# First pass of a decoder layer: scores of four heads by one product with K on a block diagonal, head average by adding transposes, dt in six buffers

## What is computed

```
x_dbl = xs @ x_proj.T;  dt, Bm, Cm = split(x_dbl)           # 64, 16, 16
dt = softplus(dt @ dt_proj.T + dt_b)                         # 512 channels
h  = exp(dt * A) * h + dt * Bm * xs;  y = sum_n h * Cm       # scan over 128 tokens, 16 states
x  = layernorm(x + (y + D * xs) * silu(z) @ out_proj.T)
Q, K = x @ Wq, ctx @ Wk                                      # 4 heads of 32
scores = where(mask, Q K^T / sqrt(32), -inf)                 # 128 x 128 per head
attn = softmax over the 32 largest of each row, 0 elsewhere
c_t = mean over heads(attn) @ ctx @ Wv ...
```

## Time and profile before

| | us |
|---|---|
| three runs | 7404.6, 7409.21, 7412.53 |
| median | 7409.21 |
| profiled execution | 7415.14 |
| its span, first to last instruction | 7413.3 |
| mean granted clock of TensorE | 0.944 |

### The profile page before, as it was taken

How to read it: one execution, slowest core, us unless ns; L and a number is a source line. 1 busy time by engine, 2 the same in 40 slices (tenths; PEclk the granted TensorE clock), 3 DMA queues, 4 the chain that set the end, 5 groups by cost and what they waited for, 6 DMA issues and landing times. The chain is left out here.

```text
span 7413.3 us, 107688 instructions
## 1 busy us (share of the span) xinstructions
PE 6760.6 (91%) x25104; PEld 3801.7 (51%) x25104; DVE 5403.0 (73%) x13960; ACT 4455.8 (60%) x9788; POOL 4601.7 (62%) x3991
## 2 busy tenths in 40 slices
PE   3899999999999999999999999996899999999996
PEld 1354455444554555544554445543656666555664
DVE  5588888888888888888888888885255555555555
ACT  2788887887878887888878888773211111111111
POOL 0888888888888888888888888883011111111111
PEclk6999999999999999999999999997899999999998
DMA  1666566555666566655666556664511111101010
GB/s 44 136 147 147 136 153 154 145 143 136 154 152 148 142 144 161 147 142 136 151 155 147 142 139 155 153 147 136 189 30 32 32 32 32 30 28 30 28 32 20
DMA packets 554213, 835.19 MB, mean 113 GB/s; under 512 B 169179, under 2 KB 207388, under 8 KB 551712
## 3 DMA queue, kind: packets, MB, share of 16 engines
q1 hardware_dynamic: 552768, 820.23, 44.7%
q10 hardware_dynamic: 864, 8.65, 0.3%
HBM read 745.91 MB, written 74.45 MB: 111 GB/s over the span
## 5 line engine op out<-in xcount | busy, mean ns | idle before, releaser
L1255 POOL TENSOR_TENSOR arena<-arena 128x512 f32<-128x512 f32 x2048 | 2592.3, 1280 | 306.6 <-DVE arena L1180 255.3
L877 PE MATMUL psum<-arena 128*128 128x512 f32 x4096 | 2165.7, 625 | 31.4 <-POOL arena L1255 25.4
L1180 DVE TENSOR_TENSOR_SCAN arena<-arena,psum 128x512 f32<-128x512 f32 x1024 | 1236.5, 1208 | 382.1 <-ACT arena L1049 295.2
L1268 POOL TENSOR_TENSOR arena<-arena 128x512 f32<-128x512 f32 x1024 | 1332.4, 1301 | 122.4 <-PE psum L877 122.2
L1036 ACT ACTIVATE arena<-arena 128x128 f32<-128x128 f32 x4096 | 1302.0, 394 | 144.8 <-PE psum L862 144.4
L1184 DVE TENSOR_TENSOR_SCAN arena<-psum,arena 128x512 f32<-128x512 f32 x1024 | 1234.5, 1206 | 87.0 <-issue 39.0
L877 PEld LDWEIGHTS psum<-arena 128*128 128x128 f32 x4096 | 705.8, 197 | 575.5 <-issue 375.3
L1827 POOL TENSOR_SCALAR arena<-arena 128x4 f32<-128x4 f32 x160 | 36.7, 229 | 1251.8 <-DVE arena L1690 1251.8
L1049 ACT ACTIVATE arena<-arena 128x508 f32<-128x508 f32 x1024 | 736.0, 719 | 57.9 <-DVE arena L1180 57.1
L862 PEld LDWEIGHTS psum<-arena 128*128 128x128 f32 x4096 | 516.6, 146 | 494.2 <-issue 437.4
L1049 ACT ACTIVATE psum<-arena 128x508 f32<-128x508 f32 x1024 | 699.8, 683 | 48.1 <-DVE arena L1180 30.7
(11 more groups left out here) (214 smaller groups left out, 10671.8 us busy)
## 6 DMA issues: line engine op xcount, KB each, us to landing
arena<-bc_scratch SPq DMA_DIRECT2D x1152, 512.0 KB, 5.3
arena<-in_xT_dram SPq DMA_DIRECT2D x32, 512.0 KB
arena<-in_x_dram SPq DMA_DIRECT2D x32, 512.0 KB, 7.7
x_scratch<-arena SPq DMA_DIRECT2D x32, 512.0 KB, 5.7
xin_scratch<-arena SPq DMA_DIRECT2D x128, 128.0 KB, 2.5
arena<-kernel_scratch SPq DMA_DIRECT2D x32, 512.0 KB, 6.4
arena<-x_scratch SPq DMA_DIRECT2D x32, 512.0 KB, 3.7
out_dram<-arena SPq DMA_DIRECT2D x32, 512.0 KB
```

Source lines behind the costliest of these rows:

```text
L877: pe.matmul(y_ps, ident, ring[:, u % RING], start=False, stop=n == NS - 1).then_inc(S["nsum"], 1)
L1180: dve.tensor_tensor_scan(s, decay_sb[:, u // 2 % 2], bx_ps[:, u // 2 % 2], 0.0, ALU.mult, ALU.add)\
L1255: pool.tensor_tensor(h, h, Cb[:, u // 2 % PAIRS, u % 2], ALU.mult).then_inc(S["hc"], 1)
L1268: pool.tensor_tensor(ring[:, u % RING], uu[par][:, c], Bb[:, state(u)], ALU.mult)\
```

## The change

K is copied in four pieces into `kz`, which for each sequence has four blocks of 128 columns with only one head's 32 rows set, the rest zero since the start (one DVE memset). Then one product of all 128 rows of Q with 512 columns gives the four heads, and one mask product runs over 512 columns too. ACT's `dg` scales `sc` in place instead of making diagonals, and PE's `at` adds four transposes. For the room, dt has six chunks: 0 and 1 are shared by both blocks. xs moves to where dt was in front. The places of many steps in the four tables change. The diff, cut to its core (left out: renamed counts in other waits and indexing by `dt(par, c)`):

```diff
...
-    xt_mm=2, x1T=2, q_mm=1, k_mm=1, qT=1, kT=1, maskb=1, s_mm=16,
-    v8=4 * KR, took=4 * KR, nmax=4, ex=4, em=4, rinv=4, rq=4, diag=4, at_mm=4, atT=4,
+    xt_mm=2, x1T=2, q_mm=1, k_mm=1, qT=1, kT=H, maskb=1, s_mm=G,
+    v8=4 * KR, took=4 * KR, nmax=4, ex=4, em=4, rinv=4, rq=4, scaled=4, at_mm=4, atT=4,
...
-PE_AT = dict(xc0=2, xc1=3, xc2=6, xc3=7, op0=8, op1=8, op2=9, op3=10, z0=13, z1=13, z2=14, x1T=17, z3=19, qk=21,
-             sc0=22, xp=24, bt=26, dt0=29, sc1=29, dt1=30, dt2=34, at0=35, dt3=36, sc2=36, at1=40, ds0=42, ds1=43,
-             ds2=44, sc3=45, at2=49, ds3=51, tu0=53, at3=53, xa=54, tu1=55, film0=56, film1=58, tu2=59, film2=60,
-             tu3=60, film3=62)
-ACT_AT = dict(xc0=5, y3=5, xc1=5, xc2=6, xc3=9, z0=12, x1=14, z1=14, z2=15, x1T=16, z3=19, qk=23, si=24, xp=26,
-              sm0=26, bt=28, dt0=31, dg0=31, dt1=33, dt2=34, sm1=36, dt3=38, at0=39, se=39, dg1=39, sl=40, at1=42,
-              sm2=44, ds0=44, ds1=46, dg2=46, ds2=48, at2=49, sm3=50, ds3=52, dg3=52, at3=53, tu0=53, xa=54, tu1=56,
-              tu2=62, tu3=63)
-DVE_AT = dict(xc0=4, xc1=4, xc2=5, xc3=6, ln1=12, ln2=18, tka0=24, tkb0=24, tkc0=24, tkd0=26, sm0=26, tka1=31,
-              tkb1=32, tkc1=33, tkd1=34, sm1=35, tka2=38, sr=38, tkb2=39, tkc2=40, tkd2=41, sm2=42, tka3=46, tkb3=47,
-              tkc3=48, tkd3=49, sm3=49, film0=57, film1=59, film2=62, film3=63)
-POOL_AT = dict(mask=4, y3=6, rs1=15, rs2=21, sp0=45, sp1=48, sp2=53, sp3=59)
+PE_AT = dict(xc0=0, xc1=2, xc2=4, xc3=6, op0=7, op1=8, op2=12, op3=13, z0=13, z1=14, z2=14, x1T=16, z3=19, qk=19,
+             sc0=23, xp=25, bt=26, dt0=28, sc1=30, dt1=32, dt2=35, dt3=37, at0=38, sc2=41, at1=42, ds0=43, ds1=44,
+             ds2=44, sc3=44, at2=49, ds3=51, tu0=53, at3=53, xa=54, film0=55, tu1=55, film1=58, tu2=60, film2=61,
+             tu3=61, film3=63)
+ACT_AT = dict(xc0=5, y3=5, xc1=5, xc2=5, xc3=8, z0=12, x1=14, z1=14, z2=15, x1T=16, z3=19, qk=23, si=24, xp=27,
+              sm0=28, bt=30, dg0=30, dt0=33, dt1=35, sm1=35, dt2=36, at0=38, dt3=38, se=39, dg1=40, sl=40, at1=41,
+              sm2=44, ds0=44, dg2=45, ds1=45, at2=48, ds2=48, sm3=50, ds3=52, dg3=52, at3=53, tu0=53, xa=54, tu1=58,
+              tu2=59, tu3=61)
+DVE_AT = dict(xc0=3, xc1=4, xc2=5, xc3=9, ln1=12, ln2=17, tka0=23, tkb0=24, tkc0=24, tkd0=26, sm0=27, tka1=32,
+              tkb1=35, tkc1=35, tkd1=38, sm1=39, sr=39, tka2=39, tkb2=39, tkc2=40, tkd2=41, sm2=42, tka3=45, tkb3=47,
+              tkc3=48, tkd3=49, sm3=49, film0=57, film1=59, film2=60, film3=62)
+POOL_AT = dict(y3=7, mask=12, rs1=15, rs2=20, sp0=46, sp1=49, sp2=52, sp3=54)
...
-    o0=("res", 1), o1=("res", 2), t0=("x1T", 1), t1=("x1T", 2), q=("qT", 1), k=("kT", 1),
+    o0=("res", 1), o1=("res", 2), t0=("x1T", 1), t1=("x1T", 2), q=("qT", 1), k=("kT", H),
...
+        kz_zero = sems.named("kz_zero")
...
-        dt, uu = [], []
+        uu, xs = [], []
...
-            dt.append(cv.f32(C * T).rearrange("p (c t) -> p c t", c=C))
...
+            xs.append(cv.f32(C * T).rearrange("p (c t) -> p c t", c=C))
+        dt6 = cv.f32((C + 2) * T).rearrange("p (c t) -> p c t", c=C + 2)
...
-        qT, kT = cv.f32(T), cv.f32(T)
+        qT = cv.f32(T)
+        kz = cv.f32(G * H * L).rearrange("p (b h g) -> p b h g", b=G, h=H)
...
-        diag = cv.f32(H * P).rearrange("p (h g) -> p h g", h=H)
...
+        def dt(par, c):
...
+            return dt6[:, c if c < C // 2 else c + C // 2 * par]
...
+        assert ACT_AT["dt0"] >= NS and ACT_AT["dt1"] >= 2 * NS
...
-            need_apart(sp, ("decay", NB - 2, C * NS), ("u", NB - 1, C), ("scan", NB - 2, C * NS), ("ut_mm", NB - 1, C))
-            need(sp, "bx", NB - 2, 32)
+            need_apart(sp, ("nsum", NB - 2, C * NS), ("bx", NB - 2, 32))
...
                         need(pe, "qT", i, 1)
-                        need(pe, "kT", i, 1)
+                        need(pe, "kT", i, H)
                         need(pe, "maskb", i, 1)
...
                         need(pe, "em", i, b)
-                    for h in range(H):
-                        rows = slice(h * HD, (h + 1) * HD)
-                        if h:
-                            need(pe, "s_mm", i, b * H + h)
-                        o, row = ps[:, h * P:(h + 1) * P], slice(h * HD, h * HD + 1)
-                        pe.matmul(o, ones[row], maskb[row, b * L:(b + 1) * L], start=True, stop=False)
-                        pe.matmul(o, qT[rows, b * L:(b + 1) * L], kT[rows, b * L:(b + 1) * L],
-                                  start=False, stop=True).then_inc(S["s_mm"], 1)
+                    pe.matmul(ps, ones[0:1], maskb[0:1, b * L:(b + 1) * L][:, None, :].to_broadcast([1, H, L]),
+                              start=True, stop=False)
+                    pe.matmul(ps, qT[:, b * L:(b + 1) * L], kz[:, b], start=False, stop=True).then_inc(S["s_mm"], 1)
                 elif name[:2] == "at":
...
                     ps = bank(f"a{b}")
-                    need(pe, "em", i, b + 1)
-                    need(pe, "diag", i, b + 1)
+                    need(pe, "scaled", i, b + 1)
                     for h in range(H):
-                        mm = pe.matmul(ps[:, 0:L], sc[:, h], diag[:, h], start=h == 0, stop=h == H - 1)
+                        mm = pe.matmul(ps[:, 0:L], sc[:, h], ident, start=h == 0, stop=h == H - 1, is_transpose=True)
                     mm.then_inc(S["at_mm"], 1)
...
                         need(act, "u", i - 2, C)
+                    if c < C // 2:
+                        need(act, "decay", i - 1, NS * (c + 1))
                     act.activation(small[:, c], tile_ps(name), ACT.Abs, bias=vec[:, V_DTB + c:V_DTB + c + 1])\
                         .then_inc(S["vabs"], 1)
-                    act.activation(dt[par][:, c], tile_ps(name), ACT.Relu, bias=vec[:, V_DTB + c:V_DTB + c + 1])\
+                    act.activation(dt(par, c), tile_ps(name), ACT.Relu, bias=vec[:, V_DTB + c:V_DTB + c + 1])\
                         .then_inc(S["vrelu"], 1)
...
                     need(act, "q_mm", i, 1)
-                    need(act, "s_mm", i - 1, G * H)
+                    need(act, "s_mm", i - 1, G)
                     act.copy(qT, tile_ps("q")).then_inc(S["qT"], 1)
                     need(act, "k_mm", i, 1)
-                    act.copy(kT, tile_ps("k")).then_inc(S["kT"], 1)
+                    for h in range(H):
+                        rows = slice(h * HD, (h + 1) * HD)
+                        act.copy(kz[rows, :, h], seqs(tile_ps("k"))[rows]).then_inc(S["kT"], 1)
                 elif name == "y3":
...
-                    if c:
-                        need(act, "at_mm", i, c)
-                    else:
-                        need(act, "at_mm", i - 1, G)
+                    need(act, "em", i, c + 1)
...
-                        a = act.activation(diag[:, h], ident, ACT.Identity, scale=rq[:, h:h + 1])
-                    a.then_inc(S["diag"], 1)
+                        a = act.activation(sc[:, h], sc[:, h], ACT.Identity, scale=rq[:, h:h + 1])
+                    a.then_inc(S["scaled"], 1)
...
+            act.wait_ge(kz_zero, 1)
...
-                        need_apart(dve, ("s_mm", i, (b + 1) * H), ("nmax", i, b))
+                        need_apart(dve, ("s_mm", i, b + 1), ("nmax", i, b))
...
-                        need_apart(dve, ("s_mm", i, H))
+                        need_apart(dve, ("s_mm", i, 1))
...
+            dve.memset(kz, 0.0).then_inc(kz_zero, 1)
...
```

More of the change, by code:

```diff
@@ L529, in pass1 @@
         tmask8, tmb = cv.u8(G), cv.f32(G)
-        xs = [cv.f32(C * T).rearrange("p (c t) -> p c t", c=C) for _ in range(2)]
         zs = [cv.f32(C * T).rearrange("p (c t) -> p c t", c=C) for _ in range(2)]
@@ L778, in step @@
                     need(pe, "vrelu", i, c + 1)
-                    pe.matmul(ps, ident, dt[par][:, c], start=False, stop=True).then_inc(S["ds_mm"], 1)
+                    pe.matmul(ps, ident, dt(par, c), start=False, stop=True).then_inc(S["ds_mm"], 1)
                 elif name[:2] == "op":
@@ L967, in step @@
                     need(act, "ds_mm", i, c + 1)
-                    act.copy(dt[par][:, c], tile_ps(name)).then_inc(S["dt"], 1)
+                    act.copy(dt(par, c), tile_ps(name)).then_inc(S["dt"], 1)
                 elif name == "x1":
@@ L1048, in iteration @@
                     decay = (decay_sb if through_pe(u) else decay_ps)[:, u // 2 % 2]
-                    act.activation(seqs(decay)[:, :, 1:L], seqs(dt[par][:, c])[:, :, 1:L],
+                    act.activation(seqs(decay)[:, :, 1:L], seqs(dt(par, c))[:, :, 1:L],
                                    ACT.Exp, scale=negA[:, c, k:k + 1]).then_inc(S["decay"], 1)
@@ L1236, in step @@
                 elif name == "mask":
-                    need_apart(pool, ("ld_mask", i, 32), ("s_mm", i - 1, G * H))
+                    need_apart(pool, ("ld_mask", i, 32), ("s_mm", i - 1, G))
                     pool.tensor_scalar(maskb, mask8, -1.0, -OFF, ALU.add, ALU.mult)\
@@ L1246, in step @@
                     need(pool, "xs", i, 1)
```

(2 more changed lines are left out.)

## The result

The changed kernel takes 7596.2 us (median of four runs, 7584.7 to 7611.4); the kernel before, run beside it, 7406.9 (7400.4 to 7412.5). The ratio is 1.0257, 95% interval 1.0236 to 1.0278: 189 us slower, where 7307 us and a gain were forecast, and outside the range. The profiled execution took 7599.5 us, its span is 7597.7, its mean clock 0.945 against 0.944 before.

A forecast was written before the change was run, and what follows sets the result against it. PE was taken to bound one half of each block, mutual waits of DVE and ACT the other. Terms (2.9 + 1.5 - 0.6 - 0.6) gave 3.2 us x 31, with the tail 102 us: median 7307 us, range 7235 to 7420.

The forecast's parts named there:

- what PE is spared there is time: Unit 50 to unit 23 of the next block, 75.5 us: PE busy 75.0 us, so work saved on it shortens the block.
- term b: Second half of block: remaining 2.9 us of PE work and a 2.32 us wait before sequence 2's scores; 1.5 us gained.
- a: PE-bound half: score products of sequences 0 and 1, head averages of 2 and 3; 2.9 us gained per block.
- Term c: ACT's four K copies ahead of the silu, less its vanished wait for K; 0.6 us lost, bounds 0 and 1.7.
- Term d: Last two output products moved to PE steps 12 and 13, delaying the norm's statistics; 0.6 us lost, bounds 0 and 1.8.
- edits with one answer: K's diagonal clearing, dt in six buffers, other moves of equal-size work by one or two units: no cost counted.
- B: Saved PE time turns into waiting for the scan: 0 to 0.7 us per block, 7385 to 7409 us; chance 0.12.
- C: DVE's step 39 gathers 7.4 us between scans, POOL starves, second half grows 4.0 us: 7477 us; chance 0.13.
- D: PE waits more often and loses its clock, up to 5 us of PE work per block: about 7412 us; chance 0.05.
- The rule on transposes: Skill's rule that 2.4 GHz doesn't engage for transposes; by it the all-transpose head average would help lose the clock.
- A: PE is the bound throughout, so all 5.8 us per block count: 183 us gained, 7226 us; chance 0.10.

The follow-up runs named there:

- one copy of K: New computation at the old places, K copied by ACT in one piece instead of four (three heads' K left out): 7357.5 us, ratio 0.9933.
- the early K: New computation at the old places, with K made and copied apart from Q in step 12, ahead of z0: 7413.8 us, ratio 1.0023.
- the first experiment: The changed computation with the four tables of places of the kernel before: 7423.6 us, ratio 1.0033.
- four tries: Changed kernel with one group back at old places: output products 7624.0 us; transposes of u and last films 7608.5; attention 7681.2; softplus 7647.9.
- the lump alone in the old places: New computation at old places, with DVE's masked scores of sequence 1, softplus addition and two top-k rounds all in step 39: 7429.3 us, ratio 1.0027.

## Why the prediction was wrong

**What failed first** is the sentence "what PE is spared there is time", read off because PE was busy for 75.0 of 75.5 us. The units of TensorE's saving were nearly right: one mask and product take 1.27 us and one average 0.44, 5.2 us less per block where 5.8 were forecast, and the pass lost about 170 us of this work. But at the old places all of it, wait of term b included, was worth 46 us (one copy of K), 1.4 us per block instead of the 4.4 of terms a and b. The averages gave 0.73 us for 1.8 us of work, the scores 0.7 for 3.4; doubling them cost 1.0 for 4.6. In the same row POOL is busy for 70.6 us, and halving part of its work took 60 us off: PE was full without being alone in setting the pace. Where added PE work did count in full is the stretch up to z, which the early K showed and where nothing was saved.

**Term c** was mis-sized, 0.6 for 2.1 us per block, above its upper bound of 1.7. The copies' length was right (2.39 us). What it set against them, the vanished wait of 1.09 us for K, is only in the new places (no bracket ahead of L989 there), and no run shows that it buys anything there. Since the four copies alone eat more than all the TensorE work they make possible, the change loses 23 us before any place is touched.

**Term d and the "edits with one answer"** failed most: 0.6 us per block for the norm and nothing for the other moves, against 60 us (1.9 per block) for the first half and 112 (3.5) for the rest. Of the first, the statistics' wait on POOL is the visible part: 4.6 us, where I bounded it by how much later DVE would end (1.8) and did not ask how far POOL would have caught up by then. It is not shown to be the cause, since it fell to a third when the output products went back and the time did not fall. The claim that the other moves cost nothing was not worked out from any row. Nor are they all moves by one or two units: POOL's mask goes from 4 to 12, its sp3 from 59 to 54, DVE's xc3 from 6 to 9. With the moves of norm and attention, the places cost 172 us.

**The rivals.** B (time goes into waits, no gain) is what the new computation does at the old places: 7424, at about 170 us less TensorE work, just beyond its 7409. C gave the right side, and its mechanism is in the trace (lump in 39, POOL idle 7.72 us where 3.97 was allowed for), but the second half of the block, which C had growing by 4.0 us, shrank by 1.4, and the lump is not the cause by itself: put in alone it costs nothing clear (6 us), and spread out it costs 123 more. That the time came out on C's side is not to its credit. D is out: the pass's clock is 0.96 as before, and the run with the clock at 0.99 was no faster. The rule on transposes that was weighed there didn't show: with the averages as transposes the pass keeps its 0.96 when nothing else is changed, and has 0.97 in the row of the first experiment. A is out by the first experiment.

**What stays open** is which moves make the 172 us. The traces say where they fall. From the kernel of the first experiment to the changed one the mean block grows by 5.8 us:

| units | new computation, old places, us | changed kernel, us |
|---|---|---|
| 0 to 20 | 46.5 | 48.7 |
| 20 to 32 | 28.9 | 27.6 |
| 32 to 44 | 34.4 | 38.1 |
| 44 to 50 | 16.4 | 17.7 |
| 50 to 56 | 9.7 | 8.2 |
| 56 to 64 | 17.1 | 18.4 |

The largest part lies in units 32 to 44, around the lump and yet not from it alone, and no group put back brought that stretch near its 34.4 (attention 38.0, softplus 40.5). Putting one group back made the kernel no better in four tries (28, 12, 85 and 52 us slower, of which 12 is near the noise), spreading the lump made it 123 slower, while going back in all takes 172 off. So the cost of the places is not a sum over single groups, which would give the wrong sign. Which pairs of moves matter was not separated.

## What to carry to other kernels

Before work saved on a full engine is counted as time, double a piece of that work or look for another engine that is as full in the same stretch; here a fifth to a quarter counted. Price the preparation that a cheaper product needs (four copies, 2.1 us) against the saving (1.4 us), on the engine that waits next. And keep a new computation and a new order apart: the new head average alone at the old places, 7374 us, is the version to keep, 0.4% under the kernel before and 2.9% under the changed one.

## What was unexpected of the hardware

In these traces the softplus addition on DVE (128 x 2048, both inputs in SBUF) and POOL's products don't run side by side: whoever starts first is spared, and the other's time grows by about the rest of it. The group of the addition in the kernel before:

```profile
L1111 DVE SCALAR_TENSOR_TENSOR arena<-arena 128x2048 f32<-128x2048 f32 x32 | 76.1, 2378 | 68.9 <-ACT arena L962 68.9
```

and in the changed kernel:

```profile
L1112 DVE SCALAR_TENSOR_TENSOR arena<-arena 128x2048 f32<-128x2048 f32 x32 | 101.5, 3173 | 44.9 <-ACT arena L963 44.9
```

It took 3.20 us where POOL's product had begun 0.22 us ahead of it (rows of the lump above). In the earlier trace rows it took 2.29, having begun 0.95 us ahead of a product on POOL, and that one took 2.47 instead of 1.27. With the lump alone in the old places two products took 4.56 instead of 2.50. The Trainium skill ("SBUF — State Buffer", "SBUF: two separate sides") calls this an exclusive lock of the port pair that the two engines share, held for the whole instruction, also for a DVE operation with two SBUF inputs; the trace agrees. So the new places also cost DVE 0.8 us per block by the moment at which the addition meets POOL, which no count of work shows.

The clock told little of the time. With the lump alone in the old places the pass ran at 0.99 instead of 0.97, and the kernel was no faster (7429 and 7424 us): in the two stretches shown TensorE was busy for 27 us less and idle for 31 more.
